# AdaLN, Mamba and mixture of experts on one core: the output stage reordered by groups of tokens, weight loads moved

## The reference

```
h = layernorm(x) * (1 + ca) + sa
u, delta, B, C, z = projections of h (u after a causal convolution of 4 taps and silu)
state[t] = exp(delta[t] * A) * state[t-1] + delta[t] * u[t] * B[t]     # 512 channels, 16 states
y[t] = sum over the states of state[t] * C[t]
x = x + ga * (((y + u * D) * silu(z)) @ Wout.T + bout)
```

```
h2 = layernorm(x) * (1 + cb) + sb
top 2 of h2 @ gate, softmax over the two -> weights
x = x + gb * sum over the two of weight * ((silu(h2 @ w0[e]) * (h2 @ w1[e])) @ wo[e])
```

## Time and profile before

| | us |
|---|---|
| median of 3 runs (lowest, highest) | 921.65 (919.79, 925.30) |
| the profiled execution's own time | 922.18 |
| its span in the profile | 920.4 |
| busy PE, DVE, POOL, ACT | 738.3, 645.6, 504.0, 322.9 |
| the same as a share of the span | 80%, 70%, 55%, 35% |
| mean granted clock of PE | 0.93 of full speed |

### The profile page before, as it was taken

How to read it: one execution, slowest core, us unless ns; L and a number is a source line. 1 busy time by engine, 2 the same in 40 slices (tenths; PEclk the granted TensorE clock), 3 DMA queues, 4 the chain that set the end, 5 groups by cost and what they waited for, 6 DMA issues and landing times.

```text
span 920.4 us, 10283 instructions
## 1 busy us (share of the span) xinstructions
PE 738.3 (80%) x2240; PEld 365.7 (40%) x2241; DVE 645.6 (70%) x878; ACT 322.9 (35%) x359; POOL 504.0 (55%) x263
## 2 busy tenths in 40 slices
PE   5899996777777877878778787875059999999994
PEld 3434342223222322323223233664026666666663
DVE  4467687989999899989989999655314444444442
ACT  1677755453454445434444542011011111111110
POOL 1000014897999999899899999207602222222222
PEclk9999997999999999999899999995569999999998
DMA  9353304656556565655555555752632222222220
GB/s 268 99 149 98 125 26 136 219 182 201 216 195 218 180 221 181 226 172 203 198 198 200 203 219 203 257 200 88 199 112 44 39 42 44 42 42 44 45 39 0
DMA packets 73060, 132.85 MB, mean 144 GB/s; under 512 B 10506, under 2 KB 46666, under 8 KB 72908
## 3 DMA queue, kind: packets, MB, share of 16 engines
q1 hardware_dynamic: 62676, 123.77, 40.2%
q0 software_dynamic: 7152, 8.48, 5.5%
q10 hardware_dynamic: 3208, 0.34, 0.3%
HBM read 93.82 MB, written 35.47 MB: 140 GB/s over the span
## 4 chain that ended last, share of the span: by engine, by line
PE 46%; DMA 15%; POOL 15%; DVE 12%; issue 7%; ACT 4%; ACTq 0%; SPq 0%; POOLq 0%; DVEq 0%
PE PS L651 15%; DMA hT<-C_scratch 13%; PE PS L449 9%; POOL pool L1307 8%; DVE pool L1041 7%; PE PS L667 7%; PE PS L548 6%; PE PS L564 3%; POOL spread L1330 3%; POOL expert_in_scratch L1354 2%; ACT PS L804 2%; PE PS L659 2%; DVE pool L1029 1%; PE PS L530 1%; PE PS L639 1%
## 5 line engine op out<-in xcount | busy, mean ns | idle before, releaser
L1307 POOL TENSOR_TENSOR pool<-pool,hT 128x1024 f32<-128x1024 f32 x128 | 299.9, 2362 | 31.6 <-PE PS L548 24.3
L548 PE MATMUL PS<-pool,ident 128*128 128x512 f32 x512 | 263.4, 639 | 61.1 <-POOL pool L1307 61.0
L1041 DVE TENSOR_TENSOR_SCAN pool<-PS,pool 128x1024 f32<-128x1024 f32 x96 | 215.7, 2274 | 0.6 <-ACT PS L804 0.6
L804 ACT ACTIVATE PS<-pool,negA 128x1024 f32 (+1 forms) x128 | 143.1, 1118 | 201.0 <-DVE pool L1041 200.9
L548 PEld LDWEIGHTS PS<-pool,ident 128*128 128x128 f32 x512 | 97.0, 199 | 171.7 <-POOL pool L1307 92.0
L1373 POOL DMA_INDIRECT out<-uT,ptab x39 | 60.6, 1553 | 184.3 <-DVE uT L1254 182.3
L651 PE MATMUL PS<-pool,uT 128*128 x312 | 142.5, 600 | 0.8 <-ACT uT L865 0.4
L1029 DVE TENSOR_TENSOR pool<-PS,pool 128x1024 f32<-128x1024 f32 x96 | 117.6, 1225 | 21.5 <-ACTq L798 6.7
L530 PE MATMUL PS<-pool 96*128 96x512 bf16 x256 | 81.7, 402 | 36.6 <-DVE pool L1029 35.0
L1228 DVE TENSOR_TENSOR uT<-uT,PS 128x512 f32<-128x512 f32 x39 | 26.9, 689 | 92.7 <-PE PS L651 89.9
L1330 POOL TENSOR_TENSOR spread<-spread,pool 128x1024 f32<-128x1024 f32 x32 | 75.5, 2361 | 27.7 <-DMA hT<-C_scratch 27.7
(11 more groups left out here) (163 smaller groups left out, 697.0 us busy)
## 6 DMA issues: line engine op xcount, KB each, us to landing
hT<-C_scratch SPq DMA_DIRECT2D x128, 512.0 KB
expert_in_scratch<-zrow SPq DMA_DIRECT2D x68, 261.0 KB, 7.6
pool<-in_w SPq DMA_DIRECT2D x16, 512.0 KB, 10.6
uT<-expert_in_scratch SPq DMA_DIRECT2D x39, 130.5 KB, 2.1
Y<-Y SPq DMA_DIRECT2D x32, 128.0 KB, 2.4
C_scratch<-Y SPq DMA_DIRECT2D x8, 512.0 KB, 2.6
Y<-in_wo SPq DMA_DIRECT2D x8, 512.0 KB, 10.6
x_tok<-in_x SPq DMA_DIRECT2D x4, 512.0 KB, 9.1
```

What stands on the lines that cost most here:

```text
L548: m = pe.matmul(PS[:, 6 + half, :], ident[:, :], prod[:, k % PR, HF * half:HF * half + HF], start=False, stop=k == DS - 1)
L804: act.activation(pair(2 * (k % 2)).unsqueeze(1), delta[:, bass.ds(g2 * 2 + r, 1), :], ACT.Exp, scale=decay[:, bass.ds(g2 * (2 * DS) + n, 1 ...
L1041: dve.tensor_tensor_scan(hst[:, k % HR, :], pair(2 * (k % 2)), driven, 0.0, ALU.mult, ALU.add).then_inc(scan_done, 1)
L1307: gp.tensor_tensor(prod[:, k % PR, :], hst[:, k % HR, :], crep[:, k % RC, :], ALU.mult).then_inc(prod_done, 1)
```

## The change

PE, DVE, ACT and POOL now take the groups one after the other. PE does tiles 3 to 7 outward at once; then for each group it transposes and computes logits, with the transpose of the next tile ahead of the logits of this one, does the first tile of the group after next outward, then the ranks, then the other three tiles outward. DVE takes group 0 as far as measured, gates two chunks, computes h2 of group 0, fills the tables' constants and gates the other two chunks; then for each group q it adds and measures group q + 1, picks, weighs and places group q, and computes h2 of group q + 1. ACT takes the exponential of a group right after its tiles. POOL does rstd of groups 0 and 1, and for groups 0 and 1 sends three of the eight DMAs, does rstd of group q + 2, and sends the other five. On SP, six of the eight loads of w0 are issued in the last pass over two chunks, each behind the fetch of C for k = 3, 7 and 11; the loads of wo follow those of w1 as soon as all chunks are gated, ahead of the stores of x.

```diff
--- before.py
+++ after.py
@@ -1,3 +1,4 @@
+import itertools
 from contextlib import ExitStack
 
 import numpy as np
@@ -342,6 +343,10 @@
                 sp.dma_start(stk[0:PARTS * 32, r, :],
                              B_dram[bass.ds(g2 * 2 + r, 1)].rearrange("g a i n -> (g a i) n")).then_inc(stk_in[r], 16)
 
+            def w0_of(e):
+                sp.wait_ge(exp_done, DS * (e + 1))
+                sp.dma_start(w0_sb[:, e], w0[e].rearrange("(k p) n -> p k n", p=P)).then_inc(w01_in, 16)
+
             def C_of(g2, last):
                 for r in range(2):
                     for k in range(DS):
@@ -351,6 +356,8 @@
                                      .unsqueeze(1).broadcast_to([HC, DS, L])).then_inc(crep_in[k % RC], 16)
                         if k % 2 == 0:
                             zeros((g2 * 2 + r) * 8 + k // 2)
+                        if last and k in (3, 7, 11):
+                            w0_of(3 * r + k // 4)
                         if k == DS // 2 and not (last and r == 1):
                             sp.wait_ge(stk_free, g2 * 2 + (r + 1))
                             B_of(g2 + r, 1 - r)
@@ -366,16 +373,18 @@
 
 
             sp.wait_ge(ysum_done, RC + NG * DS)
-            for dst, src in ((w0_sb, w0), (w1_sb, w1)):
-                for e in range(NE):
-                    sp.dma_start(dst[:, e], src[e].rearrange("(k p) n -> p k n", p=P)).then_inc(w01_in, 16)
+            w0_of(NG - 2)
+            w0_of(NG - 1)
+            for e in range(NE):
+                sp.dma_start(w1_sb[:, e], w1[e].rearrange("(k p) n -> p k n", p=P)).then_inc(w01_in, 16)
+            sp.wait_ge(gated, NG)
+            for e in range(NE):
+                sp.dma_start(wo_sb[:, e], wo[e].rearrange("(k p) n -> p k n", p=P)).then_inc(wo_in, 16)
             for q in range(NQ):
                 tiles = slice(TQ * q, TQ * q + TQ)
                 sp.wait_ge(x2_step, TQ * q + TQ)
                 sp.dma_start(out_dram[:, tiles, :], x_tok[:, tiles, :]).then_inc(x2_out, 16)
             sp.wait_ge(c_over, 3)
-            for e in range(NE):
-                sp.dma_start(wo_sb[:, e], wo[e].rearrange("(k p) n -> p k n", p=P)).then_inc(wo_in, 16)
             sp.wait_ge(sent, 16 * 2 * NT)
 
             def row_of(slot):
@@ -617,18 +626,21 @@
                         m = pe.matmul(to, w, rhs, start=n == 0, stop=n == len(parts) - 1)
                 m.then_inc(rank_mm, 1)
 
-            outward_y(TQ - 1)
-            for stage in range(NQ + 3):
-                if 0 <= stage - 3 < NQ:
-                    ranks(stage - 3)
-                for i in range(TQ):
-                    t = TQ * (stage - 1) + i
-                    if 0 <= t < NT:
-                        turn_h2(t)
-                    if stage < NQ - 1:
-                        outward_y(TQ * (stage + 1) + i)
-                    if 0 <= t < NT:
-                        logits(t)
+            for t in range(TQ - 1, 2 * TQ):
+                outward_y(t)
+            for q in range(NQ):
+                first = TQ * q
+                turn_h2(first)
+                for t in range(first + 1, first + TQ):
+                    turn_h2(t)
+                    logits(t - 1)
+                logits(first + TQ - 1)
+                if q < NQ - 2:
+                    outward_y(first + 2 * TQ)
+                ranks(q)
+                if q < NQ - 2:
+                    for t in range(first + 2 * TQ + 1, first + 3 * TQ):
+                        outward_y(t)
             pe.drain().then_inc(c_over, 1)
 
 
@@ -850,12 +862,9 @@
                 act.activation(w12[:, 1, tiles], w12[:, 0, tiles], ACT.Exp).then_inc(ex_done, 1)
 
             for q in range(NQ):
-                if q >= 2:
-                    gap_exp(q - 2)
                 for t in range(TQ * q, TQ * q + TQ):
                     take_h2(t)
-            gap_exp(NQ - 2)
-            gap_exp(NQ - 1)
+                gap_exp(q)
             act.drain().then_inc(c_over, 1)
 
 
@@ -1156,43 +1165,37 @@
                 dve.wait_ge(yev_done, 1 + c + 1)
                 dve.tensor_tensor(uT[:, c, :], uT[:, c, :], szT[:, c, :], ALU.mult).then_inc(gated, 1)
 
-            for stage in range(NQ + 3):
-                if stage < NQ:
-                    first = TQ * stage
-                    if stage == 0:
-                        gate_y(CH)
-                    added_y(first)
-                    if stage == 0:
-                        gate_y(CH + 1)
-                    added_y(first + 1)
-                    if stage == 0:
-                        gate_y(CH + 2)
-                    measured(first)
-                    added_y(first + 2)
-                    measured(first + 1)
-                    added_y(first + 3)
-                    measured(first + 2)
-                    gathered(first)
-                    measured(first + 3)
-                    for t in range(first + 1, first + TQ):
-                        gathered(t)
-                if stage == 0:
-                    gate_y(CH + 3)
-                    route_tables()
-                if 0 <= stage - 3 < NQ - 2:
-                    weights(stage - 3)
-                    place_of(stage - 3)
-                if 0 <= stage - 1 < NQ:
-                    first = TQ * (stage - 1)
-                    for t in range(first, first + TQ):
-                        centre(t)
-                    for t in range(first, first + TQ):
-                        h2_of(t)
-                if 0 <= stage - 2 < NQ:
-                    pick(stage - 2)
-                if stage >= NQ + 1:
-                    weights(stage - 3)
-                    place_of(stage - 3)
+            def residual(q):
+                first = TQ * q
+                added_y(first)
+                for t in range(first + 1, first + TQ):
+                    added_y(t)
+                    measured(t - 1)
+                measured(first + TQ - 1)
+                for t in range(first, first + TQ):
+                    gathered(t)
+
+            def normal_h2(q):
+                for t in range(TQ * q, TQ * q + TQ):
+                    centre(t)
+                for t in range(TQ * q, TQ * q + TQ):
+                    h2_of(t)
+
+            residual(0)
+            gate_y(CH)
+            gate_y(CH + 1)
+            normal_h2(0)
+            route_tables()
+            gate_y(CH + 2)
+            gate_y(CH + 3)
+            for q in range(NQ):
+                if q < NQ - 1:
+                    residual(q + 1)
+                pick(q)
+                weights(q)
+                place_of(q)
+                if q < NQ - 1:
+                    normal_h2(q + 1)
 
             step(dve.tensor_copy(cnt, PS[:, 6 + (NQ - 1) % 2, P + TQ * NE:P + TQ * NE + NE]))
             settled()
@@ -1347,21 +1350,23 @@
                 gp.wait_ge(rstd2_done, 2 * q + 1)
                 gp.tensor_tensor(rstd[:, tiles], rstd[:, tiles], nhalf[:, tiles], ALU.pow).then_inc(rstd2_done, 1)
 
-            def send(q):
-                gp.wait_ge(placed, q + 1)
-                for t in range(TQ * q, TQ * q + TQ):
-                    for i in range(2):
-                        gp.indirect_dma_start(out=xs_dram, out_offset=bass.IndirectOffsetOnAxis(ap=posu[:, i, t:t + 1], axis=0),
-                                              in_=h2row[:, t, :], in_offset=None).then_inc(sent, 16)
-
-            for q in range(NQ - 1):
-                rstd_of(q)
+            def send(q, part):
+                for t, i in list(itertools.product(range(TQ * q, TQ * q + TQ), range(2)))[part]:
+                    gp.indirect_dma_start(out=xs_dram, out_offset=bass.IndirectOffsetOnAxis(ap=posu[:, i, t:t + 1], axis=0),
+                                          in_=h2row[:, t, :], in_offset=None).then_inc(sent, 16)
+
+            rstd_of(0)
+            rstd_of(1)
             gp.wait_ge(noted, 2)
             gp.wait_ge(xs_zeroed, 16 * NZ)
-            send(0)
-            rstd_of(NQ - 1)
-            for q in range(1, NQ):
-                send(q)
+            for q in range(NQ):
+                gp.wait_ge(placed, q + 1)
+                if q < NQ - 2:
+                    send(q, slice(0, 3))
+                    rstd_of(q + 2)
+                    send(q, slice(3, 2 * TQ))
+                else:
+                    send(q, slice(0, 2 * TQ))
 
             gp.wait_ge(x2_out, 16 * 4)
             gp.sem_inc(yo_free, 2)
```

## The result

| | before | after |
|---|---|---|
| median of 20 runs, us (lowest, highest) | 922.49 (917.71, 931.25) | 912.98 (900.81, 923.46) |
| ratio, 95% interval | | 0.985 (0.983 to 0.988) |
| the profiled execution, us (its span) | 922.18 (920.4) | 918.36 (916.5) |
| forecast | | 898.5 (893 to 908) |

The change is faster by 1.5%, some 13 us by the ratio, where 23.4 us were forecast; the median lies 5 us above the range. The ratio leaves out the 8 of the new kernel's 20 runs that lie more than 1.5% above its fastest one; between the medians of all runs the gain is 9.5 us, or 1.0%. The single runs of the new kernel spread 1.7 times as far as those of the old, and the profiled execution lies 5.4 us above its median, so the trace shows the losses rather large.

The account below looks back on a forecast made before the run. The output stage was taken as one serial tail of sends on POOL, started late, before an unchanged expert loop. -21.0 (order) - 2.7 (wo) + 0.3 (w0) = -23.4 us from 922.18 gives 898.8, median 898.5, range 893 to 908.

Parts of the forecast that it names:

- Part 1: Output stage, one group at a time: first send at 600.6, last at 646.1 instead of 667.10; 21.0 us gained.
- The waits for rstd in mid-send: POOL between sends: waits 1.5 us for the third group to be measured, with five sends queued behind.
- The half-clock estimate of group 3: PE's transposes and logits of the last group, put at 1.2 GHz: 1.7 us a tile, group placed at 637.0.
- Part 3: wo loaded once gates are done: last send lands after 3.0 instead of 5.74 us; 2.7 us gained, bounds 0 and 3.0.
- Part 2: Six w0 loads in SP's queue in the last two chunks: costs 0.3 us, bounds 0 and 8.1.
- Rival C: C fetches wait for w0's whole landing; POOL loses up to 7 us six times: 940; chance 0.04.
- a last weighing later than 576 us: Sign on POOL at the end of the scans that C fetches are held up behind w0.
- A: Rival: POOL's sends slowed by DVE, all 32 at 1.31 + 0.30 us, giving 905; chance 0.12.
- stall of the length that the prediction had worked out from the rule: POOL's sends held by DVE's port: some 2.5 us for each send caught; a third of 32 would take the whole gain.
- B: Rival: PE becomes the bound, clock at 1.2 GHz from 590 on; only 4 us gained, 918; chance 0.05.
- D: Rival: moving w0 and wo fails to help, last send still lands after 5.7 us, giving 901; chance 0.09.

Follow-up runs that it names:

- e7: Changed kernel with the same six early loads of w0 issued by ACT on its own DMA queue instead of SP's; 903.49 us, ratio 0.983.
- e8: Changed kernel with the 16 stores of zeros of the last two chunks moved behind the scans, early w0 loads kept; 899.13 us, ratio 0.975.
- e3: Changed kernel with all of w0 behind the scans and wo loaded late again, so only the order is new; 911.04 us, ratio 0.989.
- e1: Changed kernel with all eight loads of w0 behind the scans again; new order and early wo stay; 903.17 us, ratio 0.975.
- e2: Kernel before with only the six loads of w0 moved into the last two chunks; 935.08 us, ratio 1.012.
- e12: Repeat of e1 (changed kernel, all of w0 behind the scans) on the chip of e9 to e11; 904.90 us, ratio 0.980.
- e9: Changed kernel with only three early loads of w0, in the last chunk but one, the other five behind the scans; 908.41 us, ratio 0.985.
- e11: Changed kernel with all w0 and 16 zeros stores behind the scans, last group's h2 before the previous group's weights and places; 898.35 us, ratio 0.974.
- e10: Word-for-word repeat of e8 (changed kernel, 16 stores of zeros behind the scans, early w0 loads kept); 905.86 us, ratio 0.982.

## Why the prediction was wrong

**Part 1, the order: right as a mechanism, 5 us short in the changed kernel's profile.** Start of the first send behind the scans' end: 19.5 forecast, 19.0 in every profile of the new order. Last send: 65.0 forecast (646.1 - 581.1); 64.5 and 65.5 in e7 and e8, whose output stage has exactly the new order, and 70.2 in the changed kernel's profile, with PE's semaphores late. The waits for rstd in mid-send came as described. The half-clock estimate of group 3 was too high (1.7 us a tile, 6.8 for four; 5.4 measured in e8), yet its places came only 0.9 us earlier than forecast there (55.0 against 55.9 us behind the scans' end), so other steps were a little longer. No send of e8 waited for these places, so neither error moved its last send.

**Part 3, wo early: right in sign and size for the landing** (3.0 us forecast, 2.6 measured, had 5.74), and silent on what it would cost to leave wo late in the new order: 8 us (e3 against e1), because the fetch of the rows suffers as well as the last send.

**Part 2, w0 in the last chunks: this is the step that failed.** I said: "Bounds: 0 (a gain is excluded, nothing here becomes shorter) and 8.1 us, six times the full transfer. I take 0.3, near the lower end". Measured: 11 us, as the part alone (e2, ratio 1.012) and as the difference of the last two chunks on POOL (109.2 us in the mean of the two kernels with all six loads and the zeros in SP's queue, 98.4 over the seven that leave w0 out of them: 10.8). By the ratios within the new order it is less, 5 to 9 us (0.985 against 0.980 in e12 and 0.975 in e1). So it is 5 to 11 us, far above the 0.3 that I took and around or above the upper bound of 8.1.

For the profiled execution the accounts close. It took 918.36 us where 898.8 were forecast for it, 19.6 more: the scans end 15.1 us later than forecast (596.5 against 581.4), the stretch from there to the first hidden product is 4.9 longer (78.4 against 73.5), the expert loop 0.5 shorter. Of the 15.1 us, 13.4 lie in the last two chunks (111.1 against 97.7). For the medians they close only roughly: the forecast with 11 instead of 0.3 is 909.2, with the 4.9 us behind the scans 914, and measured were 913.0 as the median of all runs, 909 by the ratio. (The sum itself has a slip: 898.8 less 0.5 is 898.3, not 898.5.)

Two things were wrong in the step. First, a load of 1.35 us of transfer delayed the fetches by far more: landing rose by 3.8 us (7.8 to 11.6), 2.8 times its length, in the mean of all 32 fetches, of which only six had a load right ahead of them. It is the landing alone: in every trace SP issues each of these fetches within 0.03 us of the end of the weighing that it waits for, with the loads in its queue or without. The runs show that the loads do it (e1, e2, e9), also from another queue (e7), and that taking out traffic of another kind helps (e8, e11); they do not show why. The Trainium skill (DMA: Bandwidth & Descriptors, "Latency and other measured facts") gives HBM's access latency as 0.2 us on average and 2 us at high load; the trace agrees in sign, but 3.8 us is more than that whole span (a landing is that of a whole transfer, not of one access). The same page ("Issuing engines are not separate DMA queues") has it that DMAs of different engines run on the same 16 DMA engines and interleave; e7 agrees in that the loads still hurt from ACT's queue (10.1 us).

Second, the room. The ring of four has a plain condition that I could have worked out: a fetch is issued when the weighing four places before is done, so four places can't be faster than one landing and one weighing. The kernel before takes 97.7 / 31 = 3.15 us a place, a weighing takes 2.35, so the fetches are free up to 4 x 3.15 - 2.35 = 10.3 us. They stood at 7.8 in the mean and at 9.18 on the chain: 2.5 us of room in the mean, and half of it used by the worst ones. At 11.6 us a place takes at least (11.6 + 2.35) / 4 = 3.5 us, and 111.1 / 31 is 3.6. This is a condition on means, and single fetches cross it earlier: in e8, at 10.1 us, 14 of 32 landed less than 0.2 us before use. I had read that POOL's engine "never shows an idle gap that a fetch ended" as room, where it said only that the limit had not been crossed in that stretch. And the stretch was too short. In the earlier chunks of the same trace, the same loop, the same view (120 to 466 us) has six such gaps:

```profile
POOL pool L1307 <- DMA hT<-C_scratch: 4.8, 6, 1.3
```

**Rival C** had the right place: w0 ahead of the fetches. Its price was wrong the other way, 7 us a load where it is 1.8, so it did not reach the 3.9 from which it decides, and it ended as some half of the gain lost, a middle course that neither my sum nor the rival had. The sign that I had set for it, a last weighing later than 576 us, did come: in the changed kernel's profile the last one ended at 591.4. **A**: sends beside DVE cost up to 1.28 us, but 25 of the 32 took at most 0.98; no effect on the sum. So no stall of the length that the prediction had worked out from the rule of the Trainium skill (SBUF — State Buffer, "SBUF: two separate sides") is seen: the changed kernel's trace shows 0.3 us at most, and the longest send of any run, 1.68 us in e8, 0.7. **B**: not so; PE's clock was 0.94 and 0.66 in the two parts of the stage, and the order held. **D**: not so.

The wide range of the single runs (22.7 us for the changed kernel, 13.5 for the one before, 3.3 in e11 of six runs) would fit a stage that has crossed its limit, where every late fetch is passed on. The record does not bear it out: e1, without the loads, ranges over 14.3 us in six runs, and e3, also without them, over 2.7 in five. What sets the range stays open.

## What to carry to other kernels

Before putting a transfer into a stage whose DMA share is only a half, work out the room of what is already in flight: with a ring of n buffers it is n times the stage's own pace less the time of one use, against the landing times in the trace, not against the share or against idle gaps that aren't there yet. Work that nobody waits for is best moved behind the tight stage, not into it: here, in e1, all of w0 was issued within 4.2 us behind the scans and first used 75 us later (588.7, 663.7), and leaving it there makes 2.0 to 2.5% of a change that was worth 1.5. And a tail of serial sends is shortened by starting it early, which one can follow instruction by instruction: to half a microsecond for the first send, and to 5 or 7 for the last where PE's semaphores came late.

## What the runs showed of the hardware

- Loads of 0.5 MB, three beside every 16 fetches of the same size, lengthened the landing of the fetches by 3.8 us with a DMA share of 0.60 in the stage, where each load fills the engines for 1.35 us; from another engine's queue by 2.3 us.
- Beside 4 MB of loads a store of scattered rows lands in 6.9 instead of 2.6 us, and a fetch of 0.13 MB in 4.8 instead of 2.1 us (e3 and e1).
- In nine of the fourteen traces some semaphores of PE came 1 to 5 us after the end of the product in the trace, in the other five they did not; e8 and e10 are the same program, one of each kind, and their last sends start 65.5 and 72.1 us behind the scans' end.
